# Adjacency tiles are turned as they land, with layer 0's preparation between them

## The reference

```python
wh = jnp.matmul(h_mat, weight).reshape(n, H, OUT_PER_HEAD)
logit_parent = jnp.einsum('nhf,hf->nh', wh, a_src)
logit_child = jnp.einsum('nhf,hf->nh', wh, a_dst)
e = jax.nn.leaky_relu(logit_parent[:, None, :] + logit_child[None, :, :], ALPHA)
att = jnp.where(adj[..., None] > 0, e, NEG_BIG)
att = jax.nn.softmax(att, axis=1)
h_prime = jnp.einsum('njh,jhf->nhf', att, wh)
```

## Time and profile before

| | before |
|---|---|
| median of 3 runs (lowest, highest) | 729.58 us (724.99, 729.62) |
| the profiled execution | 728.98 us |
| its span in the trace | 727.2 us |
| PE busy | 613.8 us (84%) |
| DVE busy | 522.2 us (72%) |
| ACT busy | 237.8 us (33%) |
| POOL busy | 220.3 us (30%) |

### The profile page before, as it was taken

How to read it: one execution, slowest core, us unless ns; L and a number is a source line. 1 busy time by engine, 2 the same in 40 slices (tenths; PEclk the granted TensorE clock), 3 DMA queues, 4 the chain that set the end, 5 groups by cost and what they waited for, 6 DMA issues and landing times.

```text
span 727.2 us, 15552 instructions
## 1 busy us (share of the span) xinstructions
PE 613.8 (84%) x5771; PEld 558.1 (77%) x5771; DVE 522.2 (72%) x922; ACT 237.8 (33%) x381; POOL 220.3 (30%) x160
## 2 busy tenths in 40 slices
PE   0769779999990399689888769999999999999897
PEld 0658669999990165379886469999999999999797
DVE  4765567767638536616676589999999999999811
ACT  2645001111110322356545124333333333333363
POOL 3046031111001001225351214444444444443542
PEclk9955579999985599879999779999999999999999
DMA  6766000000000000000000000000000000000001
GB/s 247 305 232 231 2 3 2 2 0 0 0 1 0 0 1 0 0 1 1 1 1 1 4 0 2 1 2 0 0 0 0 0 0 0 0 0 1 1 15 45
DMA packets 5966, 20.06 MB, mean 28 GB/s; under 512 B 416, under 2 KB 3360, under 8 KB 3872
## 3 DMA queue, kind: packets, MB, share of 16 engines
q1 hardware_dynamic: 4944, 18.88, 7.0%
q10 hardware_dynamic: 976, 0.59, 0.3%
HBM read 18.42 MB, written 1.05 MB: 27 GB/s over the span
## 4 chain that ended last, share of the span: by engine, by line
PE 28%; DVE 21%; issue 16%; DVEq 1%; ACT 1%; POOL 1%; ACTq 0%; POOLq 0%
PE bank L1052 11%; PE bank L1193 6%; PE bank L1030 6%; DVE denc L1676 5%; DVE tc L1694 4%; DVE yc L1701 3%; DVE G L1561 2%; PE bank L1203 2%; DVE h L1305 1%; PE bank L1082 1%; DVE stats L1259 1%; PE bank L1174 1%; PE bank L1071 0%; POOL rstd L518 0%; PE bank L1112 0%
## 5 line engine op out<-in xcount | busy, mean ns | idle before, releaser
L1193 PE MATMUL bank<-ATc,denc 128*128 128x128 f32 x1536 | 185.7, 278 | 15.3 <-ACT ATc L838 8.4
L1193 PEld LDWEIGHTS bank<-ATc,denc 128*128 128x128 f32 x1536 | 179.1, 194 | 17.2 <-issue 16.6
L592 POOL TENSOR_TENSOR dTc<-dTc,yc 128x512 f32<-128x512 f32 x64 | 112.5, 1757 | 163.2 <-ACT yc L832 111.5
L1052 PE MATMUL bank<-pcs,Ar 128*128 128x256 f32 x768 | 97.5, 291 | 7.1 <-DVEq L1291 3.7
L1052 PEld LDWEIGHTS bank<-pcs,Ar 128*128 128x128 f32 x768 | 96.3, 199 | 8.6 <-DVEq L1291 4.5
L830 ACT ACTIVATE yc<-bank 128x512 f32<-128x512 f32 x64 | 38.3, 598 | 163.9 <-PE bank L1193 163.9
L1676 DVE TENSOR_SCALAR denc<-cB,rc 128x2048 f32<-128x2048 f32 x48 | 85.1, 1777 | 0.3 <-DVE rc L1668 0.3
L1030 PE MATMUL bank<-pcs,A 128*128 128x385 bf16 x256 | 45.0, 338 | 28.7 <-DVEq L1284 28.7
L1203 PE MATMUL bank<-XW,yc 128*128 128x128 f32 x512 | 67.5, 275 | 1.8 <-DVE yc L1701 1.8
L1701 DVE SCALAR_TENSOR_TENSOR yc<-tc,dTc 128x512 f32<-128x512 f32 x64 | 64.6, 1028 | 0.0
L981 PEld LDWEIGHTS bank<-whp,G 128*128 128x128 bf16 x768 | 56.4, 99 | 9.8 <-issue 9.0
(11 more groups left out here) (192 smaller groups left out, 827.9 us busy)
## 6 DMA issues: line engine op xcount, KB each, us to landing
a<-in_adj SPq DMA_DIRECT2D x16, 1024.0 KB, 4.7
out<-X SPq DMA_DIRECT2D x4, 256.0 KB, 2.2
W<-in_L_gnn_W ACTq DMA_DIRECT2D x1, 192.0 KB, 6.5
attB<-in_L_gnn_att_weight ACTq DMA_DIRECT2D x1, 128.0 KB, 4.7
a3B<-in_L_gnn_a ACTq DMA_DIRECT2D x1, 128.0 KB, 7.5
W<-in_L_gnn_weight ACTq DMA_DIRECT2D x1, 64.0 KB, 2.1
W<-in_L_gnn_W ACTq DMA_DIRECT2D x1, 64.0 KB, 6.8
X<-in_x SPq DMA_DIRECT2D x1, 0.5 KB, 8.7
```

Of the source, the lines that this page charges most:

```text
L592: nc.gpsimd.tensor_tensor(own, own, yc[b][c][:, :], ALU.mult).then_inc(yd_ready, 1)
L1052: last = nc.tensor.matmul(bank[t % 2][:, 0:2 * D], Ar[t % 4][:, kt, :], pieces[:, kt, :], start=kt == 0, stop=kt == T - 1)
L1193: last = nc.tensor.matmul(bank[c][:, P * k:P * k + P], denc[b][:, part, j0:j0 + P], ATc3[b][:, part, :], start=part == 0, stop=part == NC - 1)
```

## The change

Six things change, all ahead of the choice.

1. Four landing buffers instead of two, at the cost of SBUF that is free then (`h0` moves).
2. PE turns tile `it` as soon as it is cast. The loop is written out, all 16 tiles, and the preparation is placed between tiles 0 to 6.
3. The second bank of each tile, 8 of the 16 transposes, is copied out by ACT (`second_half`) instead of DVE. ACT does this three tiles behind its casts.
4. The logits come out of the projection: DVE multiplies `W0` by the attention weights once (`w0a`), which makes 8 more columns of `W0`, and the projection matmul gives 136 columns instead of 128. The four DVE operations over 2048 columns go.
5. The projection is written in six groups of three tiles, in two banks, each copied out by three DVE copies (`projected0`).
6. DVE waits for all five weights first and does the products with them (layer 3's too) ahead of the moments.

The diff, cut to its core:

```diff
-        a32 = [at(f"a32_{b}", B + 8 * b, [P, N]) for b in range(2)]
+        a32 = [at(f"a32_{b}", B + 8 * b, [P, N]) for b in range(4)]
...
-            with sp.Fori(1, HT) as g:
-                for b in range(2):
-                    sp.wait_ge(a_ready, 2 * g + b - 1)
-                    load(2 * g + b, b)
+            with sp.Fori(1, NG) as g:
+                for b in range(4):
+                    sp.wait_ge(a_ready, 4 * g + b - 3)
+                    load(4 * g + b, b)
...
+            def second_half(it):
+
+                act.wait_ge(at_bank[1], it + 1)
+                nc.scalar.copy(AT[:, HT:T, P * it:P * it + P],
+                               bankb[2 * (it % 2) + 1][:, :].rearrange("p (j i) -> p j i", j=HT)).then_inc(at_copied[1], 1)
...
+            for it in range(4, T):
+                second_half(it - 3)
+                convert(it)
+                if it == 9:
+                    act.wait_ge(guard_ready, 1)
...
+            for it in range(T - 3, T):
+                second_half(it)
...
+            def turn_tile(it):
+
+                pe.wait_ge(a_ready, it + 1)
+                for grp in range(2):
+                    pe.wait_ge(at_copied[grp], it + 1)
+                    for k in range(HT):
+                        jt = HT * grp + k
+                        last = nc.tensor.transpose(bankb[2 * (it % 2) + grp][:, P * k:P * k + P],
+                                                   A[:, it, P * jt:P * jt + P], identb[:, :])
+                    last.then_inc(at_bank[grp], 1)
...
+            def project0(g):
+
+                if g >= 2:
+                    pe.wait_ge(wh_ready, g - 1)
+                for t in range(3 * g, min(3 * g + 3, T)):
+                    pe.wait_ge(hT_ready, t // GT + 1)
...
+            dve.wait_ge(w_loaded, 80)
+            for k in range(2):
+                then(nc.vector.tensor_tensor(w0a[:, :, :], W0[:, 0:D].rearrange("p (h f) -> p h f", h=H),
+                                             attB[:, :, F * k:F * k + F], ALU.mult))
+                then(nc.vector.tensor_reduce(W0[:, D + H * k:D + H * k + H], w0a[:, :, :], AX_X, ALU.add))
...
-                then(nc.vector.tensor_tensor(pr, WH[:, :, :, 0:F],
-                                             attB[:, :, F * k:F * k + F].unsqueeze(1).to_broadcast([P, T, H, F]), ALU.mult))
-                then(nc.vector.tensor_reduce(col[:, :, :], pr, AX_X, ALU.add))
```

More of the change, by code:

```diff
@@ L629, in _ @@
[L629 to L638, removed]
@@ L884, in _ @@
             pe.wait_ge(const_ready, 7)
-            turn_h(h0, 0, 0)
+            def turn_tile(it):
[7 more added lines that the diff above has]
+                    last.then_inc(at_bank[grp], 1)
+                pe.wait_ge(some_ready, it + 1)
+                for jt in range(T):
+                    last = nc.tensor.matmul(bank[6 + it % 2][:, jt:jt + 1], A[:, it, P * jt:P * jt + P], onesb[:, 0:1],
+                                            start=True, stop=True)
+                last.then_inc(edge_bank, 1)
@@ new lines, in turn_h @@
+            def turn_h(q):
+                pe.wait_ge(h_ready, q + 1)
+                if q >= 2:
+                    pe.wait_ge(hT_ready, q - 1)
+                for k in range(GT):
+                    last = nc.tensor.transpose(bank[4 + q % 2][:, P * k:P * k + P], h0[:, GT * q + k, :], ident[:, :])
+                last.then_inc(hT_banks, 1)
+            def project0(g):
[3 more added lines that the diff above has]
+                    pe.wait_ge(hT_ready, t // GT + 1)
+                    last = nc.tensor.matmul(bank[4 + g % 2][:, WP * (t % 3):WP * (t % 3) + WP], hT0[:, P * t:P * t + P],
+                                            W0[:, :], start=True, stop=True)
+                last.then_inc(wh_bank, 1)
@@ L886, in _ @@
+            turn_tile(0)
+            turn_h(0)
+            turn_h(1)
+            turn_tile(1)
+            turn_h(2)
+            turn_h(3)
             pe.wait_ge(w_loaded, 80)
+            pe.wait_ge(hT_ready, 3)
             for k in range(3):
[L888 removed]
+                last = nc.tensor.transpose(bank[4][:, P * k:P * k + P], W2[:, k, :], ident[:, :])
             last.then_inc(w2T_banks, 1)
+            turn_tile(2)
@@ L890, in _ @@
             pe.wait_ge(w2_ready, 1)
-            for t in range(T):
[L892 to L899, removed]
+            pe.wait_ge(w0_ready, 1)
@@ L900, in _ @@
+            pe.wait_ge(hT_ready, 4)
+            for g in range(3):
+                project0(g)
+            turn_tile(3)
+            for g in range(3, PG):
+                project0(g)
+            turn_tile(4)
+            pe.wait_ge(wh_ready, PG)
+            for t in range(T):
+                last = nc.tensor.matmul(bank[4][:, 0:H * F1], ones[:, :], WH[:, t, :, :].rearrange("p h f -> p (h f)"),
                                         start=t == 0, stop=t == T - 1)
@@ L903, in _ @@
             nc.tensor.matmul(bank[5][0:2 * H, 0:P], ext[:, :], ident[:, :], start=True, stop=True).then_inc(ext_bank, 1)
+            turn_tile(5)
             pe.wait_ge(ext_ready, 2)
             nc.tensor.matmul(bank[5][:, 0:2 * H], ones[0:2 * H, :], exd[:, :], start=True, stop=True).then_inc(ext_bank, 1)
-            pe.wait_ge(hT_ready, 4)
+            for it in range(6, T):
+                turn_tile(it)
             pe.wait_ge(wsum_ready, 1)
[L910 to L927, removed]
             pe.wait_ge(pieces0_ready, 1)
```

173 lines of the change are left out of this document (98 added, 75 removed).

## The result

| | before | after |
|---|---|---|
| median (lowest, highest) | 729.60 us (724.99, 730.05) | 710.38 us (706.51, 711.22) |
| ratio, 95% interval | | 0.974 [0.9687, 0.9793] |
| the profiled execution | 728.98 us | 710.04 us |
| flag `dense` written | 89.10 us | 70.38 us |

The kernel became faster by 19 us, where 8 had been forecast; the time lies under the range. The flag came 18.7 sooner, the profiled execution 18.9. From the flag to the end it was 728.98 - 89.10 = 639.9 before and 710.04 - 70.38 = 639.7 after. So all of it is won ahead of the choice, and more of it than expected.

What follows compares the result with a forecast made beforehand. PE's turning of 16 tiles, 2.62 us each, was taken to bound the way to the flag. With ACT pacing the end, the last `some` moves from 85.55 to 77.3, saving 8.2: 728.98 gives 720.8, range 714 to 727.

Steps and rivals of the forecast that it cites:

- The start: PE's first turn of `h0`: at 20.4 us, a delay of 3.5 from the weight products ahead of the moments.
- ACT's stand in front of the first `hT0` copy: ACT, after its second cast: stands from 17.05 to 21.5 us before copying `hT0`.
- The eviction on ACT: ACT copying 128x1024 bf16 of a tile's second bank: 1.03 us, between bounds of 0.59 and 1.90.
- ACT paces the end: Last tiles before the flag: ACT at 2.93 us a tile against PE's 2.3, last `some` at 77.3.
- the slower rival: PE's written-out code doesn't come in time: five stops of 3.76 cost 18.8 us, total 739.6; chance 0.06.
- The late weights of another rival: Ahead of the flag: weights landing 4 us later, or POOL's pieces past the flag, 722 to 726; chance 0.09.
- a tile is 2.3: PE turning one written-out tile: 1.8 us for 16 transposes plus 0.5 for edge counts; upper bound 2.62.
- I take 7.5: PE's projection in two pieces: 7.5 us, between 4.0 at the upper clock level and 8.0 at the lower.
- 5.3 for the sum: PE's sum over rows: begins at the lower clock level, 3.87 + 1.4 = 5.3 us, ending at 48.2.
- 2.93 a tile: ACT's cadence after tile 5's second bank: one eviction of 1.03 and one cast of 1.90 us per tile.
- that rule's case: Preparation stays at the lower clock level, kept there by transposes: 2.9 us later, 723.7; chance 0.15.
- the opposite one: Preparation runs at the upper clock level for all its length: 4.9 us sooner, 715.9; chance 0.17.

Runs made afterwards that it cites:

- x3: The changed kernel with ACT's half of the evictions given back to DVE, weaving kept; 703.7 us, ratio 0.9672.
- x9: x3 with tiles 6 to 15 turned in the old loop of two tiles instead of written out; 710.4 us, ratio 0.9743.
- x10: x3 with ACT's third cast ahead of the first `hT0` copy, exponentials two casts later, last quarter of POOL's pieces on DVE; 705.1 us, ratio 0.9661.
- x1: The kernel before with only its turning loop written out, two buffers, no weaving, DVE evicting both banks; 720.0 us, ratio 0.9888.
- x7: The kernel before with the turning loop written out and four landing buffers, nothing else; 709.2 us, ratio 0.973.
- x2: The changed kernel with all 16 tiles behind the preparation and both banks evicted by DVE; 707.1 us, ratio 0.9756.
- x8: The changed kernel with DVE's products of the weights put behind the moments and normalizing; 707.2 us, ratio 0.9724.
- x11: The changed kernel with the edits of x3 and x8 and ACT's third cast ahead of its first `hT0` copy; 702.6 us, ratio 0.964.

## Why the prediction was wrong

**Right.** The stage, its end and its constant: what lies behind the flag stayed (639.9 and 639.7). The start: the first turn of `h0` at 20.56 against 20.4. ACT's stand in front of the first `hT0` copy: 4.43, to 21.71, against 17.05 to 21.5. The eviction on ACT: 1.02 against 1.03. That ACT paces the end. That POOL's pieces are done just ahead of the flag: 69.46, against a flag at 70.38. No stop for code on PE of the size that the slower rival needed; the longest ahead of the flag in these runs was about 1 us (1.01 in x3). The late weights of another rival do occur, in x9 and x10, 3 late, but not in the execution of after that was profiled.

**The step that failed** is "a tile is 2.3", with "I take 7.5" for the projection and 5.3 for the sum. All three put PE at the lower level for most of the preparation, and the ground for it was the earlier trace rows: 42 us of transposes at 0.50 with PE busy 98%. I read that as a property of transposes. x1 shows that it is one of the loop: the same transposes and counts, written out, ran at 1.00. The bound was wrong as well, since the upper price of a tile was the loop's 2.62 and no lower one was given; a tile at the upper level is 1.3. PE's way to tile 5's second bank was then 41.8 instead of 50.6, 8.8 sooner: the wait for `hT0` and the first eviction 1.4 (tile 2 done at 29.4, not 30.8), projection 2.9 (4.6 from each piece's start to the next start, not 7.5), tiles 3 and 4 two times 1.0, sum 1.5, the rest tile 5 and the small matmul. ACT, which the forecast had standing for that bank from its eighth cast on, now stood 0.68.

**The smaller miss** is ACT's cadence, "2.93 a tile". The two durations are right, but the next instruction starts about 0.1 before the one ahead has ended in the rows (54.15 against 53.25 + 1.02), so a pair comes every 2.70. Eight pairs make 1.8. Both misses give 8.8 + 1.8 = 10.6, and the last `some` ended at 66.83 where 77.3 was forecast. Landing, taken as 2.75 a tile on full queues, was quicker as well, 2.42 in x3, and did not bind in after.

**The rule.** The Trainium skill, "TensorE: Matmul & The Clock Gate", Part 4, says that the transpose mode doesn't count as the engine being busy in the same way, and that the full rate doesn't engage. Rows of before seemed to agree. The runs don't bear out what I made of it, that transposes keep PE at the lower level: x7 is granted 1.00 from 48 to 60 with nothing on PE but transposes and one-column counts, and x2 through its 16 tiles in a row, 41.2 to 64.1. There the measurement decides. Whether transposes with no counts between them would lift or hold the clock, no run shows. I gave that rule's case 0.15 and the opposite one, the upper level throughout, 0.17; the latter was right in kind but its price, 4.9, left the tiles out, although they run at the same clock as what stands between them.

**What the parts are worth**, which the forecast added up as one: written-out transposes 7.0 and buffers nothing when alone, 18.5 together; weaving some 3.3 (x2 to x3); ACT's half of the evictions a loss of 6.5 (x3); the products ahead of the moments a loss of 3.2 (x8). The forecast booked that ACT "paces the end" and did not go on to ask what DVE would have paced it at. DVE's two copies take 1.29 a tile.

**Left open:** whether it is the address step itself or the slower sequence of matmuls that keeps the loop's clock down (x9 shows the loop doing it, not how), and whether the transposes or the counts lift it once they are written out. These prices are differences of flags, of one execution each, in which the start alone can move by 3.

## What to carry to other kernels

A stretch that is busy and yet at the lower clock says nothing about its operations until the way that they are issued is changed: look for register steps in the sequencer's rows, and price a tile at both levels. Two parts of a change can be worth little apart and together be worth all, so ask of every part what paces the stage once the others are in. Before work is moved to a second engine to relieve a first, compute both engines' cadence for one tile; the one that gets the work may be the one that ends the stage.

## What the runs showed of the hardware

- Transposes with an address from a register have a step of 46 ns each ahead of the weight load, and 16 take 2.17 us at a granted 1.00 and 2.21 at 0.50 (x9), against 1.05 and 1.89 written out (x1).
- Bf16 transposes written out, with one-column matmuls between the tiles and nothing else on PE, run at a granted 1.00 (x7, 48 to 60), and in a loop the grant fell from 1.00 to 0.57 with PE busy 4.00 of 4.00 (x9).
- DVE and POOL slow each other in some pairs of operations: in x11 the first of POOL's `rows` took 3.08 beside DVE's G, where two took 2.04 ahead of G in after, and G itself took 5.34 for two instead of 4.49.
